# Another order of work in the gated stage, and norms that signal each tile

## The chip, the cores and the metric

The kernel runs on one core of a Trainium2 chip. The metric is the time of one execution on the device in microseconds (us), the median of several runs; the profile is of one execution of its own. The engines are TensorE (PE, with its weight loads as PEld), VectorE (DVE), ScalarE (ACT), GpSimd (POOL) and SyncE (SP, which here only issues DMAs). Each engine works through its own instructions in the order in which the program wrote them, and a semaphore wait at the head of a queue holds everything behind it.

## The reference

Eight sequences of 512 tokens with 128 channels pass through eight sub-layers, each added to the residual stream x after a norm: a slot attention, a mixture of low-rank experts, a polar attention, the experts again, an attention by distance, a feed-forward with squared relu, an attention with a learned Gaussian gate, and the feed-forward again. The change touches the stretch between the distance attention and the gated one:

```python
x = x + attn_a(layernorm(x))            # its last step: context @ W_o.T
x = x + ffn(layernorm(x))               # r = relu(h); (r * r) @ w_proj, h has 512 channels
x = x + attn_b(layernorm(x))            # the gated attention; prepared from:
mixed_q = y @ wq + bq ; mixed_k = y @ wk + bk ; mixed_v = y @ wv + bv
glo = mean(mixed_q over tokens)
c = tanh(mixed_q @ wfq + bfq + (glo @ wfg + bfg))
P = sigmoid(sum(c * up)) * 512 ; Z = sigmoid(sum(c * uz)) * 512
G = -(j - P) ** 2 * 2 / Z ** 2
```

## The kernel before, in words

The program has three groups: a slot phase, a middle group (polar, distance), and a last group with the gated stage, the gated attention and the last phase. The **gated stage** (`GatedPhase`, by its prefix d7 and its tiles e_...) prepares the gated attention. It goes by batches: a batch is one of the 8 sequences, a [128 x 512] block of four tiles of 128 tokens. It is a software pipeline of steps s = 0 to 11: in step s each engine works on batch s with the parts of lag 0 (called b0 here), on batch s-1 with the parts of lag 1 (b1), and so on (b2, b3, b4). The functions `tensor`, `scalar`, `vector`, `gpsimd` and `store` write out the order for one step on PE, ACT, DVE, POOL and SP; that order is fixed by hand.

What happens to one batch:

- lag 0: `out.turn` (L176, four PE transposes of the context), `out.copy` (L182, ACT), `out.project` (L188, PE), `out.add` (L194, DVE, into x), then the first norm: `statistics` (L228) and `aggregate` (L235) on DVE, `scale` on POOL (L241 and L242 on [128 x 4], L245 a power, L247 the shift), `normalise` (L254, four ACT instructions), `turn` (L262, four PE transposes) and `copy` (L268, ACT).
- lag 1: `ffn.hidden` (L396, four products, one bank each), `relu` (L401, ACT), `square` (L406: blocks 0 and 1 on DVE, 2 and 3 on POOL), `ffn.project` (L414, 16 accumulated products), `ffn.add` (L421, DVE), and the second norm, `norm2`, by the same lines as the first; then `query` (L668, PE), `mix_query` (L685, ACT, with a sum over the tokens), `key` (L672) and `globals` (L723, one column), both PE.
- lag 2: `query_high` (L691), `key_high` (L702) on ACT, `global_bias` (L729), `key_rest` (L707), `query_rest` (L696), `values` (L712) on DVE, `centre` (L718), `steepness` (L741), `value` (L677), `position` (L745) on PE, `centre_tanh` (L736) and the two `middle` (L445) on ACT, the two `low` (L449) on DVE. Each splits a float32 into three bfloat16 parts; SP stores them (L1244).
- lag 3: `steep` (L752, L755), `position_tanh` (L760), `distance` (L765), `curves_high` (L779) on ACT; `curves` (L772, L774) and `curves_rest` (L784, [128 x 1536]) on DVE.
- lag 4: `middle` and `low` of the curves (L445, L449 at [128 x 1536]), and seven stores by SP (L1250 to L1256). `curves_high` of batch b waits until the stores of batch b-2 have landed.

Before the change PE's order in a step is hidden(b1), centre(b2), ffn.project(b1), out.turn and out.project(b0), steepness, value, position(b2), norm2.turn and query(b1), norm.turn(b0), key and globals(b1). Next step's hidden reads what `norm.copy` of this step wrote. The eight PSUM banks are shared by name (`Banks`): `take` makes PE wait until the readers of the bank's former use are done, and the plan lists name, bank, lag and readers in PE's order. The norm's semaphore `xn_ready` is raised once for four tiles, and PE waits for it once.

Behind the stage, the gated attention needs its stacks filled (L1489, L1625, L1641, sprinkled over steps 7, 8 and 10) and loaded (L1463). Its first work on PE is L1539, on DVE L1658.

Of the kernel before, what the change touches and what calls it, by code (L numbers as in the profile page):

```python
# [17 lines left out]
NT = T // P  # L18
# [22 lines left out]
def wait_ge(eng, sem, value):  # L41

    if isinstance(value, int) and value <= 0:
        return
    eng.wait_ge(sem, value)
# [151 lines left out]
class Norm:  # L197
# [40 lines left out]
    def scale(self, pool, b):  # L238
        u = b % 2
        pool.wait_ge(self.mv_ready, b + 1)  # L240
        pool.tensor_scalar(self.vareps[:, u, :], self.meanvar[:, u, :, 1], EPS, None, ALU.add).then_inc(self.ve_ready, 1)  # L241
        pool.tensor_scalar(self.minus_mean[:, u, :], self.meanvar[:, u, :, 0], -1.0, None, ALU.mult)  # L242
        pool.wait_ge(self.ve_ready, b + 1)
        wait_ge(pool, self.xn_ready, b - 1)
        pool.tensor_tensor(self.rstd[:, u, :], self.vareps[:, u, :], self.sv.minus_half[:, 0:NT], ALU.pow).then_inc(self.rstd_ready, 1)  # L245
        pool.wait_ge(self.rstd_ready, b + 1)
        pool.tensor_tensor(self.shift[:, u, :], self.minus_mean[:, u, :], self.rstd[:, u, :], ALU.mult).then_inc(self.shift_ready, 1)  # L247

    def normalise(self, act, b):
        u = b % 2  # L250
        act.wait_ge(self.shift_ready, b + 1)
        wait_ge(act, self.turned, b - 1)
        for t in range(NT):
            last = act.activation(self.xn[:, u, t, :], self.sv.x[:, b * NT + t, :], ACT.Identity,  # L254
                                  bias=self.shift[:, u, t:t + 1], scale=self.rstd[:, u, t:t + 1])
        last.then_inc(self.xn_ready, 1)

    def turn(self, pe, b):
        pe.wait_ge(self.xn_ready, b + 1)
        to = self.banks.take(pe, self.bank, b)  # L260
        for t in range(NT):
            last = pe.transpose(to[:, t * P:(t + 1) * P], self.xn[:, b % 2, t, :], self.sv.ident[:, :])  # L262
        last.then_inc(self.turned, 1)

# [6 lines left out]
class Experts:  # L271
# [95 lines left out]
        last.then_inc(self.lora_done, 1)  # L367

    def bias(self, pool, b):
        pool.wait_ge(self.norm.xn_ready, b + 1)  # L370
        x = x_tiles(self.sv, b)
        pool.tensor_tensor(x, x, self.sv.base_bias[:, :].unsqueeze(1).to_broadcast([P, NT, D]), ALU.add).then_inc(self.bias_added, 1)

# [714 lines left out]
class GatedPhase:  # L1088
# [4 lines left out]
    def __init__(self, nc, sv, tag, wo, early, late, psum):  # L1093
        self.sv = sv
        out = self.out = OutProjection(early, sv, f"{tag}_o", wo)
        ffn_norm = Norm(early, sv, f"{tag}_n", "xnT", out.added)
        ffn = self.ffn = SquaredRelu(early, sv, f"{tag}_f", ffn_norm, last_hidden=1)
        norm, norm2 = self.norm, self.norm2 = ffn_norm, Norm(early, sv, f"{tag}_m", "xnT2")
        prep = self.prep = PrepareGated(late, sv, f"{tag}_p", norm2, early)
        norm2.x_ready = ffn.x_done  # L1100
        self.place = (4, 5, 6, 7, 0, 1, 2, 3)
        banks = self.banks = Banks(nc, tag, 8, (
            ("h2", 4, 1, (ffn.relu_done[2],)), ("h0", 2, 1, (ffn.relu_done[0],)), ("h3", 5, 1, (ffn.relu_done[3],)), ("h1", 3, 1, (ffn.relu_done[1],)),
            ("c", 5, 2, (prep.cT_ready,)), ("o", 1, 1, (ffn.x_done,)), ("ctx", 0, 0, (out.ctxT_ready,)), ("out", 1, 0, (out.added,)),
            ("z", 6, 2, (prep.ez_ready,)), ("v", 4, 2, (prep.v_ready,)), ("p", 7, 2, (prep.th_ready,)), ("xnT2", 0, 1, (norm2.xnT_ready,)),
            ("q", 2, 1, (prep.q_ready,)), ("xnT", 0, 0, (norm.xnT_ready,)), ("k", 3, 1, (prep.k_split.rest_ready,)), ("g", 5, 1, (prep.gb_ready,))), tensors=[psum[:, i, :] for i in self.place])
        out.banks = norm.banks = norm2.banks = ffn.banks = prep.banks = banks

    def bank_done(self, eng, place):
# [22 lines left out]
    def tensor(self, pe, s):  # L1132
        out, norm, norm2, ffn, prep = self.out, self.norm, self.norm2, self.ffn, self.prep
        for b in batch(s, 1):
            ffn.hidden(pe, b, 2)
            ffn.hidden(pe, b, 0)
            ffn.hidden(pe, b, 3)
            ffn.hidden(pe, b, 1)
        for b in batch(s, 2):
            prep.centre(pe, b)  # L1140
        for b in batch(s, 1):
            ffn.project(pe, b)
        for b in batch(s, 0):
            out.turn(pe, b)
            out.project(pe, b)
        for b in batch(s, 2):
            prep.steepness(pe, b)
            prep.value(pe, b)
            prep.position(pe, b)
        for b in batch(s, 1):  # L1150
            norm2.turn(pe, b)
            prep.query(pe, b)
        for b in batch(s, 0):
            norm.turn(pe, b)
        for b in batch(s, 1):
            prep.key(pe, b)
            prep.globals(pe, b)

    def scalar(self, act, s):
# [6 lines left out]
        for b in batch(s, 1):  # L1166
            ffn.relu(act, b, 2)
            ffn.relu(act, b, 0)
            ffn.relu(act, b, 3)
            ffn.relu(act, b, 1)  # L1170
        for b in batch(s, 3):
            prep.position_tanh(act, b)
            prep.distance(act, b)
        for b in batch(s, 2):
            prep.centre_tanh(act, b)
            prep.q_split.middle(act, b)
            prep.k_split.middle(act, b)
        for b in batch(s, 3):
            prep.curves_high(act, b)
        for b in batch(s, 0):  # L1180
            out.copy(act, b)
        for b in batch(s, 4):
            prep.c_split.middle(act, b)
        for b in batch(s, 1):
            norm2.normalise(act, b)
            norm2.copy(act, b)
        for b in batch(s, 0):
            norm.normalise(act, b)
        for b in batch(s, 1):
            prep.mix_query(act, b)  # L1190
        for b in batch(s, 0):
            norm.copy(act, b)

    def vector_start(self, dve):
        out, norm, norm2, ffn, prep = self.out, self.norm, self.norm2, self.ffn, self.prep
# [2 lines left out]
    def vector(self, dve, s):  # L1198
# [6 lines left out]
            ffn.square(dve, b, 1)  # L1205
        for b in batch(s, 2):
            prep.query_rest(dve, b)
        for b in batch(s, 3):
            prep.curves(dve, b)
        for b in batch(s, 2):  # L1210
            prep.q_split.low(dve, b)
            prep.k_split.low(dve, b)
        for b in batch(s, 1):
            ffn.add(dve, b)
            norm2.statistics(dve, b)
            norm2.aggregate(dve, b)
        for b in batch(s, 0):
            out.add(dve, b)
            norm.statistics(dve, b)
            norm.aggregate(dve, b)  # L1220
        for b in batch(s, 2):
            prep.values(dve, b)
        for b in batch(s, 3):
            prep.curves_rest(dve, b)
        for b in batch(s, 4):
# [1 line left out]

    def gpsimd(self, pool, s):
        out, norm, norm2, ffn, prep = self.out, self.norm, self.norm2, self.ffn, self.prep
        for b in batch(s, 1):  # L1230
            norm2.scale(pool, b)
        for b in batch(s, 0):
            norm.scale(pool, b)
            ffn.square(pool, b, 2)
            ffn.square(pool, b, 3)

# [1748 lines left out]
```

## Time and profile before

| | |
|---|---|
| median of 3 runs | 1828.64 us (1828.11 to 1833.12) |
| the profiled execution | 1834.62 us, of which the profile's span is 1832.8 us |
| mean granted TensorE clock | 0.929 of full |
| gated stage in the trace | 1174.3 us (first transposes) to 1370.7 us (first L1539); DVE begins on the attention at 1385.7 us |
| busy over the whole span | PE 88%, ACT 71%, DVE 67%, POOL 20% |

Times in the rows are microseconds from the start of the span. A row of the timeline gives the start, the time from the first start to the last end, the engine, line, operation, output<-inputs, and how many instructions were merged; in brackets, how long the engine was idle before them and who released it. A row of the windows gives the stretch, its length, then the busy time of PE, PEld, DVE, ACT and POOL, each with its number of instructions, the granted TensorE clock (1.00 is 2.4 GHz, 0.50 is 1.2 GHz), the DMA share and GB/s.

### The profile page before, as it was taken

How to read it: one execution, taken by the hardware profiler on the slowest of the kernel's cores; microseconds unless marked ns; L12 is line 12 of the kernel's file. 1: busy time of each engine (PE TensorE's matmuls, PEld its weight loads, DVE VectorE, ACT ScalarE, POOL GpSimd, SP SyncE). 2: the span in 40 equal slices, each digit the busy share in tenths (PEclk: the TensorE clock that was granted, in tenths of full speed). 3: DMA queues.
4: the chain of work that ended last, by engine and by line, in shares of the span. 5: the costliest groups of instructions: out<-in, count | busy, mean ns of one | idle time of the engine just before them, and what ended most of it. 6: DMA issues, size and time to landing. Idle time of an engine off the chain costs nothing. (4 is left out here: it accounts for less than half of the span.)

```text
span 1832.8 us, 39127 instructions
## 1 busy us (share of the span) xinstructions
PE 1614.7 (88%) x14558; PEld 777.7 (42%) x14558; DVE 1233.8 (67%) x2503; ACT 1296.0 (71%) x2201; POOL 364.1 (20%) x660
## 2 busy tenths in 40 slices
PE   7899996865899999986989999777766999999988
PEld 4676674751233333345633333255431333333356
DVE  4777777799899999947611111146668999999743
ACT  4655643784688888864789999657763888888863
POOL 3422423631000000013300000023330000000153
PEclk9899896985899999998989999889976999999999
DMA  4000000055222222200131111002233222222101
GB/s 123 1 1 1 1 1 1 1 159 173 67 71 77 79 75 71 71 2 10 57 87 57 57 57 56 1 18 62 83 101 88 63 60 56 61 61 61 29 7 41
DMA packets 115392, 98.51 MB, mean 54 GB/s; under 512 B 26762, under 2 KB 105412, under 8 KB 115204
## 3 DMA queue, kind: packets, MB, share of 16 engines
q1 hardware_dynamic: 114148, 95.68, 18.5%
q8 instruction: 117, 1.92, 0.4%
q14 instruction: 71, 0.58, 0.1%
q10 hardware_dynamic: 1056, 0.33, 0.1%
HBM read 63.82 MB, written 31.59 MB: 52 GB/s over the span
## 5 line engine op out<-in xcount | busy, mean ns | idle before, releaser
L1613 ACT ACTIVATE m_probs<-m_psum 128x512 f32<-128x512 f32 (+1 forms) x768 | 513.8, 758 | 98.1 <-PE m_psum L1530 92.6
L1613 ACT ACTIVATE e_probs<-e_psum 128x512 f32<-128x512 f32 x512 | 277.2, 597 | 84.3 <-PE e_psum L1530 78.6
L1658 DVE TENSOR_REDUCE a_minus_max<-m_psum 128x1 f32<-128x512 f32 x512 | 316.1, 682 | 17.8 <-PE m_psum L1539 12.5
L1658 DVE TENSOR_REDUCE a_minus_max<-e_psum 128x1 f32<-128x512 f32 x512 | 316.1, 682 | 12.7 <-PE e_psum L1539 6.7
L1530 PE MATMUL m_psum<-m_q_stack,m_k_stack 114*32 114x512 bf16 (+1 forms) x4096 | 295.4, 385 | 13.8 <-issue 7.1
L1550 PE MATMUL m_psum<-m_probs,m_v_ones 128*32 128x512 f32 x2048 | 271.0, 601 | 2.3 <-ACT m_probs L1613 1.6
L1530 PEld LDWEIGHTS m_psum<-m_q_stack,m_k_stack 114*32 114x32 bf16 (+1 forms) x4096 | 102.1, 96 | 218.9 <-issue 124.0
L1530 PE MATMUL e_psum<-e_q_stack,e_k_stack 126*32 126x512 bf16 x2048 | 158.4, 385 | 4.6 <-issue 2.5
L1502 POOL CAST a_max_parts<-a_minus_max 128x16 bf16<-128x16 f32 x64 | 12.6, 196 | 657.2 <-DVE a_minus_max L1658 657.2
L1550 PE MATMUL e_psum<-e_probs,e_v_ones 128*32 128x512 f32 x1024 | 133.3, 595 | 0.9 <-ACT e_probs L1613 0.8
L1539 PE MATMUL m_psum<-m_k_stack,m_q_stack 48*128 48x512 bf16 x512 | 113.3, 400 | 17.1 <-DVE a_minus_max L1658 17.0
L1539 PE MATMUL e_psum<-e_k_stack,e_q_stack 60*128 60x512 bf16 x512 | 113.0, 398 | 17.0 <-DVE a_minus_max L1658 16.8
L1603 DVE COPY m_ctxT<-m_psum 128x512 f32<-128x512 f32 x16 | 11.1, 691 | 173.0 <-PE m_psum L1550 173.0
L1530 PEld LDWEIGHTS e_psum<-e_q_stack,e_k_stack 126*32 126x32 bf16 x2048 | 43.4, 95 | 109.7 <-ACT e_probs L1613 63.4
L1550 PEld LDWEIGHTS m_psum<-m_probs,m_v_ones 128*32 128x32 f32 x2048 | 51.7, 110 | 69.0 <-ACT m_probs L1613 45.8
L1539 PEld LDWEIGHTS e_psum<-e_k_stack,e_q_stack 60*128 60x128 bf16 x512 | 29.5, 94 | 116.5 <-DVE a_minus_max L1658 88.4
L1539 PEld LDWEIGHTS m_psum<-m_k_stack,m_q_stack 48*128 48x128 bf16 x512 | 29.5, 94 | 115.5 <-DVE a_minus_max L1658 86.7
L1884 POOL TENSOR_TENSOR s_rope_product<-s_qkv,rope 128x512 f32<-128x512 f32 x32 | 40.3, 1287 | 158.6 <-ACT s_qkv L1849 158.6
L1495 POOL COPY m_v_ones<-vtok 128x128 f32<-128x128 f32 x64 | 18.6, 291 | 238.8 <-PE m_psum L1550 238.6
L1669 DVE RECIPROCAL m_inv<-m_psum 128x32 f32<-128x32 f32 x32 | 11.3, 352 | 59.2 <-PE m_psum L1558 59.2
L254 ACT ACTIVATE e_q_stack<-x,e_v_ones 128x128 f32<-128x128 f32 x64 | 26.3, 482 | 33.9 <-POOL e_v_ones L247 33.9
L2172 ACT ACTIVATE s_o<-s_bank 128x512 f32<-128x512 f32 x8 | 4.8, 597 | 59.8 <-PE s_bank L2165 59.8
(427 smaller groups left out, 2763.7 us busy)
## 6 DMA issues: line engine op xcount, KB each, us to landing
polar_q<-m_late SPq DMA_DIRECT2D x24, 256.0 KB, 3.0
polar_k<-m_late SPq DMA_DIRECT2D x24, 256.0 KB, 3.4
m_q_stack<-polar_q SPq DMA_DIRECT2D x64, 96.0 KB, 2.3
m_k_stack<-polar_k SPq DMA_DIRECT2D x64, 96.0 KB, 2.3
m_q_stack<-dist_parts SPq DMA_DIRECT2D x192, 32.0 KB
m_k_stack<-dist_parts SPq DMA_DIRECT2D x192, 32.0 KB
gate_parts<-e_late SPq DMA_DIRECT2D x24, 256.0 KB, 3.0
e_q_stack<-gate_parts SPq DMA_DIRECT2D x64, 72.0 KB
```

What stands on the lines that cost most here:

```text
L254: last = act.activation(self.xn[:, u, t, :], self.sv.x[:, b * NT + t, :], ACT.Identity, bias=self.shift[:, u, t:t + 1], scale=self.rstd[:, ...
L1495: pool.tensor_copy(self.buf.v_ones[n % 2][:, :, :, 16 * (n % 2):16 * (n % 2) + DH], self.sv.vtok[:, tiles_of(b), g * GW:(g + 1) * GW].rear ...
L1502: pool.tensor_copy(self.max_parts[:, 0, :], self.minus_max[n % 2][:, :]).then_inc(self.hi_ready, 1)
L1530: last = pe.matmul(self.ps_s[i % self.PAIRS][r:r + 32, j, :], self.buf.k_stack[g][0:self.rows, h, c * P + r:c * P + r + 32], self.buf.q_st ...
L1539: pe.matmul(to[:, :], self.buf.q_stack[g][part, h, t * P:(t + 1) * P], self.buf.k_stack[g][part, h, :], start=True, stop=True).then_inc(se ...
L1550: last = pe.matmul(self.ps_pv[32 * h:32 * h + self.buf.VW, :], self.buf.v_ones[m % 2][:, c, h, :], self.buf.probs[(NT * m + c) % self.buf. ...
L1603: copied = eng.tensor_copy(self.buf.ctxT[m // 2 % 2][:, :], self.ps_pv[:, :])
L1613: act.activation(self.buf.probs[(NT * m + c) % self.buf.PROBS][:, self.WIDE * part:self.WIDE * (part + 1), :], self.ps_s[i % self.PAIRS], ...
L1658: dve.tensor_reduce(self.minus_max[n % 2][:, k:k + 1], ps[:, :], AX.X, ALU.max, negate=True).then_inc(self.bank_free, 1)
L1669: dve.reciprocal(inv[:, :, :, :], raw[:, :, :, :, DH]).then_inc(self.inv_ready, 1)
L1884: pool.tensor_tensor(self.products[n][:, :, :, :], halves[:, :, :, i, :], table, ALU.mult).then_inc(self.rope_steps, 1)
L2172: act.activation(self.o2[b % 2][:, :], self.banks.of("o")[:, :], ACT.Square).then_inc(self.o2_ready, 1)
```

## The change

`Norm.normalise` raises `xn_ready` after each of the four tiles, and `Norm.turn` takes its bank first and waits for each tile before its transpose; the two other waits on `xn_ready` count by four. This holds for every norm of this class, in the last phase and the middle group too. `Norm.scaled` is new: a DVE wait for the shift. The rest is in `GatedPhase`:

- PE: out.turn(b0) and centre(b2) and then out.project(b0) stand ahead of ffn.project(b1); value ahead of steepness; query behind norm.turn.
- ACT: out.copy(b0) directly behind the relus; centre_tanh between position_tanh and distance; norm.normalise(b0) behind curves_high, ahead of the curves' middle(b4) and of norm2.normalise(b1); norm.copy ahead of mix_query.
- DVE: out.add, statistics, aggregate(b0) ahead of curves(b3) and of ffn.add(b1); key's low behind values and behind the new wait for norm2's shift, ahead of curves_rest.
- POOL: norm.scale(b0) ahead of norm2.scale(b1).
- Banks: "out" moves from bank 1 to 6 (behind z), "xnT" from bank 0 to 1 (behind o), and the plan follows PE's new order.

```diff
     def normalise(self, act, b):
         u = b % 2
         act.wait_ge(self.shift_ready, b + 1)
         wait_ge(act, self.turned, b - 1)
         for t in range(NT):
-            last = act.activation(self.xn[:, u, t, :], self.sv.x[:, b * NT + t, :], ACT.Identity,
-                                  bias=self.shift[:, u, t:t + 1], scale=self.rstd[:, u, t:t + 1])
-        last.then_inc(self.xn_ready, 1)
+            act.activation(self.xn[:, u, t, :], self.sv.x[:, b * NT + t, :], ACT.Identity,
+                           bias=self.shift[:, u, t:t + 1], scale=self.rstd[:, u, t:t + 1]).then_inc(self.xn_ready, 1)
 
     def turn(self, pe, b):
-        pe.wait_ge(self.xn_ready, b + 1)
         to = self.banks.take(pe, self.bank, b)
         for t in range(NT):
+            pe.wait_ge(self.xn_ready, NT * b + t + 1)
             last = pe.transpose(to[:, t * P:(t + 1) * P], self.xn[:, b % 2, t, :], self.sv.ident[:, :])
+    def scaled(self, dve, b):
+        dve.wait_ge(self.shift_ready, b + 1)
...
@@ GatedPhase.tensor
+        for b in batch(s, 0):
+            out.turn(pe, b)
         for b in batch(s, 2):
             prep.centre(pe, b)
+        for b in batch(s, 0):
+            out.project(pe, b)
         for b in batch(s, 1):
             ffn.project(pe, b)
-        for b in batch(s, 0):
-            out.turn(pe, b)
-            out.project(pe, b)
         for b in batch(s, 2):
+            prep.value(pe, b)
             prep.steepness(pe, b)
-            prep.value(pe, b)
             prep.position(pe, b)
         for b in batch(s, 1):
             norm2.turn(pe, b)
-            prep.query(pe, b)
         for b in batch(s, 0):
             norm.turn(pe, b)
         for b in batch(s, 1):
+            prep.query(pe, b)
             prep.key(pe, b)
             prep.globals(pe, b)
@@ GatedPhase.scalar
+        for b in batch(s, 0):
+            out.copy(act, b)
         for b in batch(s, 3):
             prep.position_tanh(act, b)
+        for b in batch(s, 2):
+            prep.centre_tanh(act, b)
+        for b in batch(s, 3):
             prep.distance(act, b)
...
         for b in batch(s, 3):
             prep.curves_high(act, b)
         for b in batch(s, 0):
-            out.copy(act, b)
+            norm.normalise(act, b)
         for b in batch(s, 4):
             prep.c_split.middle(act, b)
         for b in batch(s, 1):
             norm2.normalise(act, b)
             norm2.copy(act, b)
         for b in batch(s, 0):
-            norm.normalise(act, b)
+            norm.copy(act, b)
         for b in batch(s, 1):
             prep.mix_query(act, b)
-        for b in batch(s, 0):
-            norm.copy(act, b)
@@ GatedPhase.vector
         for b in batch(s, 2):
             prep.query_rest(dve, b)
+        for b in batch(s, 0):
+            out.add(dve, b)
+            norm.statistics(dve, b)
+            norm.aggregate(dve, b)
         for b in batch(s, 3):
             prep.curves(dve, b)
         for b in batch(s, 2):
             prep.q_split.low(dve, b)
-            prep.k_split.low(dve, b)
         for b in batch(s, 1):
             ffn.add(dve, b)
             norm2.statistics(dve, b)
             norm2.aggregate(dve, b)
-        for b in batch(s, 0):
-            out.add(dve, b)
-            norm.statistics(dve, b)
-            norm.aggregate(dve, b)
         for b in batch(s, 2):
             prep.values(dve, b)
+        for b in batch(s, 1):
+            norm2.scaled(dve, b)
+        for b in batch(s, 2):
+            prep.k_split.low(dve, b)
         for b in batch(s, 3):
             prep.curves_rest(dve, b)
@@ GatedPhase.gpsimd
+        for b in batch(s, 0):
+            norm.scale(pool, b)
         for b in batch(s, 1):
             norm2.scale(pool, b)
         for b in batch(s, 0):
-            norm.scale(pool, b)
             ffn.square(pool, b, 2)
             ffn.square(pool, b, 3)
```

## Rows read from the trace of the kernel before

**Rows 1.** Windows: steps 1, 2, 5 and 8 of the gated stage.
```profile
1185.05:1208.45 23.40, 17.08 (x66) 10.43 (x67) 5.34 (x20) 8.69 (x19) 5.41 (x10) 0.72 0.00 0
1208.45:1228.26 19.81, 16.70 (x82) 10.31 (x82) 8.81 (x26) 11.88 (x23) 5.41 (x10) 0.96 0.15 41
...
1271.17:1292.33 21.16, 16.07 (x84) 9.95 (x82) 14.31 (x30) 15.90 (x29) 7.87 (x10) 1.00 0.28 80
...
1335.72:1361.82 26.10, 18.12 (x67) 10.95 (x66) 14.10 (x23) 15.25 (x26) 7.98 (x8) 0.77 0.34 98
```

**Rows 2.** Timeline of step 5, PE, from the batch's hidden on.
```profile
1271.17 3.68 PE L396 MATMUL e_psum<-e_k_stack,ffn_fc 128*128 128x512 f32 x8
1274.90 1.10 PE L718 MATMUL e_psum<-e_probs,l1b_w 128*128 128x512 f32 x2
1276.99 3.81 PE L414 MATMUL e_psum<-ffn_proj,e_probs 128*128 128x128 f32 x32 [0.99 <-DVE e_probs L406]
1280.64 0.60 PE L176 MATMUL e_psum<-ident,ctx 128*128 128x128 f32 x4
1281.92 1.16 PE L188 MATMUL e_psum<-l1a_wo,e_ctxT 128*128 128x128 f32 x8 [0.69 <-ACT e_ctxT L182]
...
1286.49 0.66 PE L262 MATMUL e_psum<-ident,e_q_stack 128*128 128x128 f32 x4 [0.80 <-ACT e_q_stack L254]
1287.84 1.13 PE L668 MATMUL e_psum<-e_k_stack,l1b_w 128*128 128x512 f32 x2 [0.69 <-ACT e_k_stack L268]
1290.83 0.66 PE L262 MATMUL e_psum<-ident,e_q_stack 128*128 128x128 f32 x4 [1.87 <-ACT e_q_stack L254]
```

**Rows 3.** Timeline of the same step, ACT; the last row is of the next step.
```profile
1284.79 1.65 ACT L254 ACTIVATE e_q_stack<-x,e_v_ones 128x128 f32<-128x128 f32 x4 [1.55 <-POOL e_v_ones L247]
...
1287.19 0.60 ACT L268 ACTIVATE e_k_stack<-e_psum 128x512 f32<-128x512 f32 x1 [0.74 <-PE e_psum L262]
...
1289.13 1.65 ACT L254 ACTIVATE e_q_stack<-x,e_v_ones 128x128 f32<-128x128 f32 x4 [1.35 <-POOL e_v_ones L247]
1290.69 0.67 ACT L685 ACTIVATE pope_table<-e_psum,l1b_b 128x512 f32<-128x512 f32 x1
...
1294.37 2.28 ACT L401 ACTIVATE e_probs<-e_psum 128x512 f32<-128x512 f32 x4
```

**Rows 4.** Timeline of the same step, DVE and POOL.
```profile
1277.42 0.68 DVE L772 TENSOR_TENSOR e_late<-e_late 128x512 f32<-128x512 f32 x1
...
1280.84 0.69 DVE L421 TENSOR_TENSOR x<-e_psum,x 128x512 f32<-128x512 f32 x1 [0.81 <-PE e_psum L414]
...
1282.47 0.38 DVE L235 BATCH_NORM_AGGREGATE e_v_ones<-e_v_ones 128x2 f32<-128x6 f32 x4
...
1283.44 1.04 POOL L245 TENSOR_TENSOR e_v_ones<-e_v_ones,minus_half 128x4 f32<-128x4 f32 x1
...
1284.56 0.20 POOL L247 TENSOR_TENSOR e_v_ones<-e_v_ones 128x4 f32<-128x4 f32 x1
...
1285.62 1.75 DVE L784 TENSOR_TENSOR e_late<-e_late 128x1536 f32<-128x1536 f32 x1
1285.72 2.54 POOL L245 TENSOR_TENSOR e_v_ones<-e_v_ones,minus_half 128x4 f32<-128x4 f32 x1
```

**Rows 5.** Timeline of the tail: PE, ACT, DVE and SP, one engine after another.
```profile
1342.49 5.44 PE L414 MATMUL e_psum<-ffn_proj,e_probs 128*128 128x128 f32 x32 [1.00 <-DVE e_probs L406]
...
1357.48 2.07 PE L668 MATMUL e_psum<-e_k_stack,l1b_w 128*128 128x512 f32 x2 [0.69 <-ACT e_k_stack L268]
...
1379.04 1.48 ACT L779 ACTIVATE e_late<-e_late 128x1536 bf16<-128x1536 f32 x1 [6.92 <-DMA gate_parts<-e_late]
...
1371.61 1.75 DVE L449 TENSOR_TENSOR e_late<-e_late 128x1536 bf16<-128x1536 f32 x1
...
1373.39 1.81 SPq L1250 DMA_DIRECT2D gate_parts<-e_late  x3
```

**Rows 6.** Windows, PE alone: a stretch of step 6 with a lower clock.
```profile
1311.00:1315.50 4.50, 3.51 (x9) 0.64 0.64 197
```

More of the change, by code:

```diff
@@ L243, in scale @@
         pool.wait_ge(self.ve_ready, b + 1)
-        wait_ge(pool, self.xn_ready, b - 1)
+        wait_ge(pool, self.xn_ready, NT * (b - 1))
         pool.tensor_tensor(self.rstd[:, u, :], self.vareps[:, u, :], self.sv.minus_half[:, 0:NT], ALU.pow).then_inc(self.rstd_ready, 1)
@@ L369, in bias @@
     def bias(self, pool, b):
-        pool.wait_ge(self.norm.xn_ready, b + 1)
+        pool.wait_ge(self.norm.xn_ready, NT * (b + 1))
         x = x_tiles(self.sv, b)
@@ L1102, in __init__ @@
         banks = self.banks = Banks(nc, tag, 8, (
[L1103 to L1106, printed above, removed]
+            ("h2", 4, 1, (ffn.relu_done[2],)), ("h0", 2, 1, (ffn.relu_done[0],)), ("h3", 5, 1, (ffn.relu_done[3],)), ("h1", 3, 1, (ffn.relu_done[1],)), ("ctx", 0, 0, (out.ctxT_ready,)), ("c", 5, 2, (prep.cT_ready,)), ("out", 6, 0, (out.added,)), ("o", 1, 1, (ffn.x_done,)), ("v", 4, 2, (prep.v_ready,)), ("z", 6, 2, (prep.ez_ready,)), ("p", 7, 2, (prep.th_ready,)), ("xnT2", 0, 1, (norm2.xnT_ready,)), ("xnT", 1, 0, (norm.xnT_ready,)), ("q", 2, 1, (prep.q_ready,)), ("k", 3, 1, (prep.k_split.rest_ready,)), ("g", 5, 1, (prep.gb_ready,))), tensors=[psum[:, i, :] for i in self.place])
         out.banks = norm.banks = norm2.banks = ffn.banks = prep.banks = banks
@@ L1170, in scalar @@
             ffn.relu(act, b, 1)
+        for b in batch(s, 0):
+            out.copy(act, b)
         for b in batch(s, 3):
             prep.position_tanh(act, b)
+        for b in batch(s, 2):
+            prep.centre_tanh(act, b)
+        for b in batch(s, 3):
             prep.distance(act, b)
         for b in batch(s, 2):
-            prep.centre_tanh(act, b)
             prep.q_split.middle(act, b)
```

## The prediction

> **What bounds the kernel now.** I read the windows by step first, then one steady step on every engine, then the chain's end of the stage.
>
> The gated stage is about 200 of 1834 us, and the change's own work is all in it. [rows 1] show that no engine is full there: in step 5, at a full granted clock of 1.00 (2.4 GHz), PE is busy 16.07 us of 21.16, ACT 15.90, DVE 14.31, POOL 7.87. So the step is a chain of waits, not an engine's throughput. I count t from the start of hidden (1271.17). The chain in [rows 2 to 4], for batch b1: ffn.project runs from t = 5.82 (1276.99), when the squares are done, ffn.add starts at 9.67, aggregate ends at 11.68, POOL has the shift at 13.59 (1284.56 + 0.20), normalise runs 13.62 to 15.27, the four transposes start at 15.32, norm2.copy runs 16.02 to 16.62. I call the end of norm2.copy T.
>
> Then comes what the step pays for b0. After T the next hidden starts only at 21.16, which is T + 4.54. In between, the first norm's normalise starts at 17.96 (1289.13) because its POOL scale, second in POOL's queue, took 2.54 us for the power instead of 1.04 [rows 4]; its transposes start at 19.66 with PE idle for 1.87 us before them [rows 2]; mix_query stands behind that normalise on ACT and starts only at 19.52 [rows 3]. Query itself was done at about 17.8. The reader is to see two norms run one behind the other where b0's has no need to wait for b1's.
>
> **The change part by part.**
>
> **1. PE's detour ahead of ffn.project (a loss).** PE finishes hidden at 3.73 (next start, [rows 2]), then transposes the context (0.60) and runs centre (1.10): free at about 5.3. The relus of a step start 2.04 after hidden (1294.37, hidden at 1292.33) and take 2.28, so out.copy (0.60, the duration of the L268 row of the same shape) follows at 4.3 to 4.9. Out.project (1.16, pitch to the next 1.0) then holds PE to 6.1 to 6.3, against 5.82 where the squares are ready. I take +0.3 for ffn.project; ends 0 and 0.5. Its cover is squaring, which is the later event today.
>
> **2. DVE's order (a loss for b1).** Squares end at 5.7, query_rest (0.7) at 6.3. Out.add needs out.project (6.3); add, statistics, aggregate take 2.01 (1280.84 to 1282.85, [rows 4]) and end at 8.35. Curves are two instructions of 0.7 (0.68, [rows 4]), 9.75; the query's low 0.65, 10.4. Only then ffn.add: 10.4 against 9.67, aggregate ends at 12.4, POOL's 1.82 (12.5 to 14.3) gives norm2's shift at 14.3, against 13.59. With project at +0.5 the queue is still the later of the two, so this term is +0.7 either way.
>
> **3. POOL and the shared reads.** Norm.scale(b0) now runs from 8.45, beside the curves and a low, which all read two SBUF tensors. [rows 4] price that: the same power instruction takes 1.04 beside DVE's work from PSUM and statistics, and 2.54 when it starts 0.1 after L784, a DVE instruction with two SBUF operands. Without a conflict the shift is there at 8.35 + 0.1 + 1.82 = 10.3. At worst its reads get through only when the low ends at 10.4, then 0.95 for the power and 0.2: 11.7. In return DVE could slip a little. I take 11.7, the row that is nearest. The new DVE wait (scaled) keeps key's low, curves_rest and the curves' low away from norm2.scale. Behind that wait on DVE are 0.65 + 1.7 + 1.7 us, from 14.3 to about 18.3; the next thing DVE has to do (global_bias) cannot come before the next step, so the wait is covered by 1 us. Should that cover go, global_bias and with it the bank of h3 come late. SP's six stores of q and k then wait for key's low (15.0 instead of about 9) and go before the seven of the curves; those end near t = 4 of the next step and curves_high, which needs them, is at 9.8, so this costs nothing.
>
> The Trainium skill (SBUF — State Buffer, "Who interferes with whom") says that a DVE instruction with two SBUF inputs and a GpSimd instruction that reads SBUF exclude each other for the whole of whichever came first. The 2.54 agrees. By this rule the first scale ends at 11.7; read without it, at 10.3, and the period below would be 0.4 shorter.
>
> **4. ACT's order.** Curves_high starts when the curves are there, 9.8, with pitch 1.4: 11.2. Norm.normalise(b0) then starts at 11.7 (or 11.2), four tiles with pitch 1.56 in all: 13.25; the curves' middle 1.4: 14.65. So norm2.normalise(b1) starts at 14.65 (or 14.3, bound by POOL), against 13.62: +1.0, the largest loss.
>
> **5. Signals by tile (a gain).** From the start of four transposes to norm2.copy it is 0.70; with three done ahead, the last needs about a quarter of the 0.66, so 0.35. Gain 0.35. I give three more signals on ACT nothing: the relus signal each and run at a pitch of 0.56. In the middle group and the last phase norms are not at the head of the chain; nothing there.
>
> So T = 16.62 + 1.0 - 0.35 = 17.3.
>
> **6. Behind T (the gain).** Norm.turn has run before T. Query starts at T + 0.05 and takes 1.13, mix_query starts at T + 1.25 and signals after its sum at about T + 2.0; key is done by then; globals, and hidden at T + 2.25, not T + 4.54. ACT has norm.copy (0.5 pitch) before mix_query, in the shadow of query. The next relus start 3.68 - 0.5 = 3.2 after mix_query, 0.1 later against hidden than now. Period: 17.3 + 2.25 + 0.1 = 19.6 instead of 21.16, saving 1.55.
>
> **7. Steps of another kind.** Step 0 has only the signals by tile; the core comes there from a wait, and at half the clock (1.2 GHz) the 0.35 doubles: 0.7. Step 1 (23.40, clock 0.72) has no curves, low or middle; project is 0.9 or more late, tiles give 0.4 back, the two norms no longer queue: 1.0. Step 2 (19.81): T unchanged, hidden 2.25 behind it instead of 3.1: 1.1. Steps 3 to 7: 5 x 1.55 = 7.8. Step 8 (26.10, clock 0.77) has no b0. There norm2's scale met L784 too, costing about 2.0 with its shift instruction; PE then idled, and query ran at 2.07 instead of 1.13 [rows 5], and project took 5.44 instead of 3.81 at a lowered clock. The wait `scaled` takes the 2.0 away. Of the slow clock (1.6 + 0.9) I count on half, and ACT's middle no longer matters: 4.2 for this step up to its mix_query; ends 2.5 and 5.6.
>
> **8. Tail.** DVE reaches the attention at 1385.7 through curves_high of batch 7 (1379.04), which waited for the stores of batch 5, issued from 1373.39 behind a low at 1371.61 [rows 5]. That low waited behind values, and values behind steepness on PE. With value ahead of steepness it can be 1.3 us earlier; but the q and k stores, which now wait for key's low, keep SP busy to about 0.8 before today's. Gain 0.8; ends 0 and 2.
>
> **Sum:** 0.7 + 1.0 + 1.1 + 7.8 + 4.2 + 0.8 = 15.6 us. Against the profiled execution: 1834.62 - 15.6 = 1819.0. That execution is 6 us above the median of the runs; I take the 15.6 off the median, 1828.64: **1813.0**.
>
> **The rivals.**
>
> **A, the losses are mostly avoided (1807).** First scale not held up (period 19.2, 5 x 2.0), step 8 at full clock (5.6), tail 2: 0.7 + 1.3 + 1.4 + 10 + 5.6 + 2 = 21. For: PE idles less in all (16.1 of 19.6). Against: the 2.54 row.
>
> **B, the queues in front of norm2.normalise cost more (1821).** If POOL's conflict holds each of the four small instructions for one DVE instruction, or DVE is held by POOL in return, norm2.normalise slips by another 0.7: 5 x 0.85 = 4.3, steps 0 to 2 1.4, step 8 at slow clock 2, tail 0: 7.7. For: three in-order queues (DVE, POOL, ACT) now put b0 ahead of the critical b1. Against: each has slack of 0.3 to 0.5 in the walk above. If it slips by 1.5, the change gives nothing in steps 3 to 7 and the total is within 0.3%.
>
> **C, slower: the clock falls in the new gap (1836).** PE is done with position at about 12.9 and gets norm2's first tile at 15.1, one gap of 2.2 us where there were 0.8 and 1.87. In step 6 the granted clock was 0.64 right behind a gap of 1.87 [rows 6]. If it fell there in every step, query and key would take 2.07 each [rows 5], so that hidden comes 2.0 later, and hidden would be stretched like project (5.44 for 3.81), by 1.6: 3.6 us a step. Steps 2 to 7 then lose 3.6 - 1.55 = 2.05 each, 12.3, less 0.7 + 1.0 + 2.5 + 0.8 = 5.0 elsewhere: +7.3. It decides from a cost of about 2.4 a step. For: that step 6. Against: step 6 lost only 1.2 us, step 5 had the same gap at 1.00, and PE's busy share rises from 76 to 82%.
>
> The Trainium skill (TensorE: Matmul & The Clock Gate, Part 1) says that the engine's clock is at half unless recent activity released it; every step would be C if that gap were enough. Step 5's 1.00 speaks against it.
>
> **How the numbers follow.** Forecast 0.55, A 0.14, B 0.20 (of it 0.06 within 0.3%), no visible change for other reasons 0.04, C 0.07. A measurement of this kernel tells 0.3% (5.5 us) from no change: faster 0.83, same 0.10, slower 0.07. The range reaches from a little beyond A, 1804, to beyond B, 1823; what lies outside is C, no change, and a tail of A.
>
> **What would show it.** Steady step (hidden to hidden) 19.6 us; ffn.project about 6.1 after hidden; norm2.normalise about 14.6; norm.turn already run before norm2.copy's end; hidden 2.25 behind that end; the first L245 of a step near 2 us or more, the second 1.04; step 8 near 22 with its L245 at 1.04; attention's first L1658 some 15 us earlier. Wrong, if norm2.normalise starts past 16, if PE's clock is below 0.9 in steps 3 to 7, or if the gain of the stage is lost in the attention behind it.

## The result and the profile after

The changed kernel takes 1816.64 us (median of 5 runs, 1812.31 to 1817.17) against 1833.12 us (1828.11 to 1837.67) for the kernel before in the same comparison: a ratio of 0.991, with a 95% interval of 0.9886 to 0.9935. The profiled execution took 1817.17 us (span 1815.4), the one before 1834.62. The forecast was a gain of 15.6 us; the medians differ by 16.5, the profiled executions by 17.45. As a time it was 1813.0, counted from a median of 1828.64; in this comparison the kernel before stands 4.5 us higher, and the changed one 3.6 above the forecast. Two executions of the study, one of the kernel before (2896.83 us) and one of the kernel with query's low moved (3026.01 us), stand far above all others and are left out of every figure below.

A table of the same marks in both traces, from starts in the timeline (hidden to hidden; step 8 to the last centre; tail from there to DVE's first reduction for the attention):

| | step 0 | 1 | 2 | 3 | 4 | 5 | 6 | 7 | 8 | tail | stage |
|---|---|---|---|---|---|---|---|---|---|---|---|
| before | 10.77 | 23.40 | 19.81 | 21.99 | 20.92 | 21.16 | 22.32 | 21.07 | 26.10 | 23.87 | 211.4 |
| after | 10.30 | 21.52 | 19.96 | 20.15 | 20.43 | 20.42 | 20.42 | 20.42 | 19.97 | 25.39 | 199.0 |
| gain | 0.5 | 1.9 | -0.1 | 1.8 | 0.5 | 0.7 | 1.9 | 0.7 | 6.1 | -1.5 | 12.4 |

Of the 17.45 us, 12.4 are in the stage. The stage also began 5.2 us earlier (1169.0 instead of 1174.3), and behind it the two traces agree to 0.3 us (447.4 and 447.1). The nine kernels profiled here with the changed kernel's code ahead of the stage reached it between 1163.7 and 1170.3, a scatter of 6.6 us, and the profiled execution of before was itself 1.5 us over the median of its own comparison and 4.7 over that of the next. But that scatter lies in the first 800 us alone, and the 5.2 us can be taken apart. The marks are the first context transposes of the distance stage (PE, L176) and the first copy of the distance attention (DVE): in the kernel before, in the changed one, and in the changed one when PE waits for all four tiles at once (its experiment follows).

```profile
797.53 0.66 PE L176 MATMUL m_psum<-ident,ctx 128*128 128x128 f32 x4
941.16 0.69 DVE L1603 COPY m_ctxT<-m_psum 128x512 f32<-128x512 f32 x1 [20.96 <-PE m_psum L1550]
...
794.72 0.66 PE L176 MATMUL m_psum<-ident,ctx 128*128 128x128 f32 x4
935.91 0.69 DVE L1609 COPY m_ctxT<-m_psum 128x512 f32<-128x512 f32 x1 [21.06 <-PE m_psum L1556]
...
793.13 0.66 PE L176 MATMUL m_psum<-ident,ctx 128*128 128x128 f32 x4
936.74 0.69 DVE L1609 COPY m_ctxT<-m_psum 128x512 f32<-128x512 f32 x1 [20.90 <-PE m_psum L1556]
```

From mark to mark it is 143.63 us before, 141.19 changed and 143.61 without the waits by tile; in all ten kernels that have them it is 141.1 to 141.7. From the second mark to the gated stage it is 233.1 in all twelve. So 2.4 of the 5.2 us are a gain of the signals by tile in the distance stage. The other 2.8 stand before the first mark, which the nine kernels with the same code reach between 789.1 and 795.9, and can't be told from scatter. I count 12.4 + 2.4 = 14.8 as the change's.

The windows of the changed kernel, steps 1, 2, 5 and 8 and the tail, answer to [rows 1] (the same columns):

```profile
1179.34:1200.86 21.52, 16.15 (x66) 10.13 (x67) 5.36 (x20) 8.42 (x18) 5.41 (x10) 0.75 0.00 0
1200.86:1220.82 19.96, 17.58 (x84) 10.72 (x82) 8.78 (x26) 12.60 (x24) 5.75 (x10) 0.91 0.15 41
...
1261.40:1281.82 20.42, 17.53 (x81) 10.81 (x82) 13.95 (x30) 15.79 (x29) 6.83 (x10) 0.92 0.29 83
...
1322.66:1342.63 19.97, 15.77 (x65) 9.07 (x66) 13.23 (x23) 14.60 (x25) 5.93 (x8) 0.93 0.40 113
1342.63:1368.00 25.37, 6.36 (x18) 3.35 (x18) 14.26 (x16) 15.90 (x20) 2.95 (x6) 0.63 0.44 127
```

Steps 4 to 7 now have the same length, but at a granted clock of 0.92 where step 5 was at 1.00; PE is busy 17.53 us for the work that took 16.07. The timeline of step 5 (t from 1261.40), the PE rows that answer to [rows 2]:

```profile
1261.40 3.79 PE L398 MATMUL e_psum<-e_k_stack,ffn_fc 128*128 128x512 f32 x8
...
1266.36 1.16 PE L188 MATMUL e_psum<-l1a_wo,e_ctxT 128*128 128x128 f32 x8
1267.35 3.74 PE L416 MATMUL e_psum<-ffn_proj,e_probs 128*128 128x128 f32 x32
...
1272.68 1.02 PE L747 MATMUL e_psum<-e_probs,l1b_up 128*128 128x512 f32 x2
1276.23 1.83 PE L264 MATMUL e_psum<-ident,e_q_stack 128*128 128x128 f32 x8 [2.53 <-ACT e_q_stack L257]
1278.31 1.73 PE L670 MATMUL e_psum<-e_k_stack,l1b_w 128*128 128x512 f32 x2 [0.25 <-ACT e_k_stack L270]
1279.83 1.92 PE L674 MATMUL e_psum<-e_k_stack,l1b_w 128*128 128x512 f32 x2
1281.53 0.42 PE L725 MATMUL e_psum<-e_late,l1b_w 128*128 128x1 f32 x2
1281.82 3.81 PE L398 MATMUL e_psum<-e_k_stack,ffn_fc 128*128 128x512 f32 x8
```

The eight transposes of both norms (L264) are one row: norm.turn directly behind norm2.turn. Query and key, 1.13 and 1.02 at the full clock, take 1.73 and 1.92 behind the gap of 2.53 us. The POOL and ACT rows of the same step, for [rows 3, 4]; L245 is the power, L257 normalise, L447 (1.47) the curves' middle:

```profile
1269.66 0.58 POOL L241 TENSOR_SCALAR e_v_ones<-e_v_ones 128x4 f32<-128x4 f32 x1 [3.33 <-DVE e_v_ones L235]
...
1270.31 0.64 POOL L242 TENSOR_SCALAR e_v_ones<-e_v_ones 128x4 f32<-128x4 f32 x1
...
1270.92 1.44 POOL L245 TENSOR_TENSOR e_v_ones<-e_v_ones,minus_half 128x4 f32<-128x4 f32 x1
...
1272.68 1.65 ACT L257 ACTIVATE e_q_stack<-x,e_v_ones 128x128 f32<-128x128 f32 x4 [0.29 <-POOL e_v_ones L247]
...
1273.99 1.04 POOL L245 TENSOR_TENSOR e_v_ones<-e_v_ones,minus_half 128x4 f32<-128x4 f32 x1
1274.23 1.47 ACT L447 ACTIVATE e_late<-e_late 128x1536 bf16<-128x1536 f32 x1
...
1275.61 1.63 ACT L257 ACTIVATE e_q_stack<-x,e_v_ones 128x128 f32<-128x128 f32 x4
```

The first scale is held up in three instructions (0.58, 0.64, 1.44 for 0.24, 0.23, 1.04), the second in none. Norm2's normalise (1275.61) stands directly behind the middle, and its shift had been ready since 1275.30.

### The profile page after: what moved, and what is told of

The parts are those of the page before. It is cut to its first block and busy times, and to the rows that moved or that the text cites. A ratio compares the mean times of both kernels' runs of the same rounds, so it can differ in the third digit from the quotient of the medians.

```text
span 1815.4 us, 39134 instructions
## 1 busy us (share of the span) xinstructions
PE 1620.8 (89%) x14558; PEld 777.5 (43%) x14558; DVE 1233.2 (68%) x2503; ACT 1295.1 (71%) x2201; POOL 359.2 (20%) x660
## 3 DMA queue, kind: packets, MB, share of 16 engines
q8 instruction: 117, 1.92, 0.4%
## 5 line engine op out<-in xcount | busy, mean ns | idle before, releaser
L1664 DVE TENSOR_REDUCE a_minus_max<-e_psum 128x1 f32<-128x512 f32 x512 | 316.0, 684 | 13.2 <-PE e_psum L1545 11.7
L1536 PE MATMUL m_psum<-m_q_stack,m_k_stack 114*32 114x512 bf16 (+1 forms) x4096 | 295.3, 385 | 14.8 <-issue 6.9
L1675 DVE RECIPROCAL m_inv<-m_psum 128x32 f32<-128x32 f32 x32 | 11.3, 354 | 58.9 <-PE m_psum L1564 58.9
L257 ACT ACTIVATE e_q_stack<-x,e_v_ones 128x128 f32<-128x128 f32 x64 | 26.3, 481 | 22.7 <-POOL e_v_ones L247 22.7
```

Source lines behind the costliest of these rows:

```text
L1536: last = pe.matmul(self.ps_s[i % self.PAIRS][r:r + 32, j, :], self.buf.k_stack[g][0:self.rows, h, c * P + r:c * P + r + 32], self.buf.q_st ...
L1664: dve.tensor_reduce(self.minus_max[n % 2][:, k:k + 1], ps[:, :], AX.X, ALU.max, negate=True).then_inc(self.bank_free, 1)
```

## The experiments

**The two halves of the change.** One kernel has the signals alone (against the kernel before; the instruction's operands and the waits that count by four are left out here):

```diff
-        last.then_inc(self.xn_ready, 1)
+            act.activation(...).then_inc(self.xn_ready, 1)
+            pe.wait_ge(self.xn_ready, NT * b + t + 1)
```

> The kernel before with one part of the change alone: each of the four tiles signals and the transposes wait tile by tile, in every norm of this class; the order of the gated stage is the old one. Theory (the signals shorten each norm by 0.35 us at the head of a chain, nothing outside the gated stage): the gated stage, first context transposes to the attention's first DVE reduction, shrinks from 211.4 by 2 to 4 us, the stretch ahead of the stage stays at 1174 within its own scatter of a few us. Rival (the 5.2 us by which the changed kernel reached the stage earlier came from the signals in the slot and middle groups): the stage starts at about 1169 here too, and the total is 7 to 9 us below before.

The other has the new order alone (against the changed kernel):

```diff
     def turn(self, pe, b):
+        pe.wait_ge(self.xn_ready, NT * (b + 1))
         to = self.banks.take(pe, self.bank, b)
         for t in range(NT):
-            pe.wait_ge(self.xn_ready, NT * b + t + 1)
```

> The changed kernel, but PE waits for all four tiles before the first transpose; the new order alone. Theory: the gated stage is 3 to 4 us longer than the 199.0 of the changed kernel (0.4 in each of eight steps, since norm2's transposes then start 1 us later and end 0.35 later), and a steady step takes 20.8 instead of 20.42. Rival (the transposes spread over the normalise are what keep or lose TensorE's clock): the step changes by more than 0.6 either way, and the granted clock of the query with it.

Measured: signals alone 1825.94 us, ratio 0.997 (0.9958 to 0.9981), stage 209.1; order alone 1823.12 us, ratio 0.9953 (0.9937 to 0.9969), stage 202.0 with steady steps of 20.5. The stage's gains of 2.3 and 9.4 add up to 11.7 of the 12.4, but the 2.3 is not 0.35 a step. In the old order the signals gave 5.9 us in steps 0, 1, 2 and 8, and steps 3 to 7 became 3.6 us longer together, at granted clocks of 0.87 to 0.93 where the kernel before had 0.94 to 1.00. Its step 5:

```profile
1263.20 4.19 PE L395 MATMUL e_psum<-e_k_stack,ffn_fc 128*128 128x512 f32 x8
...
1279.46 1.12 PE L667 MATMUL e_psum<-e_k_stack,l1b_w 128*128 128x512 f32 x2 [0.69 <-ACT e_k_stack L267]
1281.71 1.54 PE L261 MATMUL e_psum<-ident,e_q_stack 128*128 128x128 f32 x4 [1.13 <-ACT e_q_stack L254]
1283.05 1.92 PE L671 MATMUL e_psum<-e_k_stack,l1b_w 128*128 128x512 f32 x2
...
1285.04 5.21 PE L395 MATMUL e_psum<-e_k_stack,ffn_fc 128*128 128x512 f32 x8
```

Query starts 16.26 behind hidden, 0.41 earlier than in [rows 2], but key takes 1.92 instead of 1.02 and the next hidden comes 5.58 behind query instead of 4.49. In the new order the signals give nearly nothing in a steady step (20.52 against 20.42) and 2.05 in step 8, 0.9 in step 1.

The first kernel reached the stage at 1168.1, the second at 1169.9. By these two starts alone the rival on the 5.2 us can't be judged; by the stretch of the distance stage it is right for 2.4 us, and the theory's "nothing outside the gated stage" is wrong: that stretch is 141.16 with the signals alone and 143.61 with the order alone. For the second the stage came out 3.0 longer as expected, but the 20.8 for its step was wrong: its queries take 2.07 where the changed kernel's take 1.73, so the two differ in the clock as well as in the signals, and neither my theory nor its rival names how the clock divides a step.

**The norm put back.** This undoes one move of the order, on ACT:

```diff
         for b in batch(s, 3):
             prep.curves_high(act, b)
-        for b in batch(s, 0):
-            norm.normalise(act, b)
         for b in batch(s, 4):
             prep.c_split.middle(act, b)
         for b in batch(s, 1):
             norm2.normalise(act, b)
             norm2.copy(act, b)
         for b in batch(s, 0):
+            norm.normalise(act, b)
             norm.copy(act, b)
```

> The changed kernel with one thing undone on ACT: the first norm's normalise stands behind norm2's copy again, not behind curves_high. Theory (the gain of the order is that b0's normalise and transposes are done before norm2's copy): norm2.normalise starts 0.4 earlier (13.8 after hidden), but after the copy query waits for 1.6 + 0.35 of norm and transposes; the step is 1 to 2 us longer than 20.42 with the clock as it is, about as long as before the change (21.2 to 22), stage about 209. Rival (the gain came from the context's projection moved ahead of the feed-forward's product): the step stays within 0.4 of 20.42.

Measured: 1829.32 us, ratio 0.9997 (0.9986 to 1.0008), stage 212.1, 3 us more than expected, steady steps 22.1 to 22.3. With everything else in place the stage's gain is gone, so the rival falls. This kernel does not price the projection's move alone, since query here also waits for the first norm's transposes, which it did not before the change; it shows that the other moves are worth nothing without b0's normalise in a time in which ACT would wait. Part of its loss can be the clock: key takes 1.46 to 1.92 in its steady steps.

**The new wait on DVE.** The call of `norm2.scaled` is left out; what it kept apart may meet.

```diff
         for b in batch(s, 2):
             prep.values(dve, b)
-        for b in batch(s, 1):
-            norm2.scaled(dve, b)
         for b in batch(s, 2):
             prep.k_split.low(dve, b)
```

> The changed kernel without DVE's new wait for norm2's shift. Theory (the wait keeps DVE's instructions with two SBUF inputs away from norm2's scale on POOL): key's low and curves_rest then run beside it, its power takes 2 to 2.8 us instead of 1.04, norm2's normalise starts 1 to 2 us later, a steady step takes 21.5 to 22.5 instead of 20.42, stage 199.0 + 7 to 12. Rival (the shared reads do not matter where ACT is the later): norm2.normalise is already 0.5 us behind its shift, so the step moves by less than 0.5.

Measured: 1820.65 us, ratio 0.9942 (0.9924 to 0.996), stage 203.2: 4.2 us longer, steady steps 20.8 to 21.8. The right sign, below the expected 7 to 12; steps 3 to 7 lose 3.9, step 8 loses 2.4 and the tail gains 2.4. Its POOL rows for norm2's scale:

```profile
1275.16 1.48 POOL L245 TENSOR_TENSOR e_v_ones<-e_v_ones,minus_half 128x4 f32<-128x4 f32 x1
1276.71 0.76 POOL L247 TENSOR_TENSOR e_v_ones<-e_v_ones 128x4 f32<-128x4 f32 x1
```

The power costs 0.44 more and the shift 0.56 more, not the 1.0 to 1.8 I had taken from the 2.54 of [rows 4]: first comes key's low of 0.69, not a DVE instruction of 1.75. What an instruction on POOL loses is what is left of the DVE instruction it meets. Norm2.normalise had 0.3 of slack, so some 0.7 a step is what one expects, and 0.35 to 1.36 is what the five steps show.

**The gap and the clock.** TensorE repeats the position product in the gap ahead of norm2's transposes, into the same bank with the same operands, twice:

```diff
     def position(self, pe, b):
         to = self.banks.take(pe, "p", b)
+        for _ in range(2):
+            pe.matmul(to[:, :], self.sv.l1b_up[:, 0, :], self.cT[b % 2][:, :], start=True, stop=True)
         pe.matmul(to[:, :], self.sv.l1b_up[:, 0, :], self.cT[b % 2][:, :], start=True, stop=True).then_inc(self.p_done, 1)
```

> The changed kernel with two repeats of the position product ahead of the real one (same operands, same bank), which fill 1.7 of the 2.53 us in which TensorE waits ahead of norm2's transposes. Theory (the gap costs the clock: query 1.73 instead of 1.13, key 1.91 instead of 1.02): the clock stays at 1.00, the end of norm2's copy to the next hidden shrinks from 3.56 to about 2.3, a steady step takes 19.2, total 6 to 9 us below the changed kernel. Rival (the clock falls whatever stands there): step unchanged at 20.4 and total within 2 us, or slower by what the repeats delay.

and once, with `range(1)`:

> The changed kernel with one repeat of the position product, which fills 0.86 of the 2.53 us gap and leaves 1.67. Theory (the gap ahead of norm2's transposes decides on the clock, and one of 1.7 is short enough, as the gaps of 1.9 of the kernel before mostly were): step 19.3 as with two repeats. Rival (any gap over about one microsecond costs the clock here): query 1.5 or more in most steps, step 20 or more.

Measured with two: 1810.79 us, ratio 0.9887 (0.9866 to 0.9908), stage 192.8, steady steps 19.04 to 19.29. With one: 1817.3 us, ratio 0.9917 (0.9902 to 0.9932), stage 199.1, steady steps 20.43. The PE timelines, two repeats:

```profile
1268.18 1.83 PE L264 MATMUL e_psum<-ident,e_q_stack 128*128 128x128 f32 x8 [0.94 <-ACT e_q_stack L257]
1270.26 1.12 PE L670 MATMUL e_psum<-e_k_stack,l1b_w 128*128 128x512 f32 x2 [0.25 <-ACT e_k_stack L270]
1271.22 1.02 PE L674 MATMUL e_psum<-e_k_stack,l1b_w 128*128 128x512 f32 x2
```

and one repeat:

```profile
1273.90 1.83 PE L264 MATMUL e_psum<-ident,e_q_stack 128*128 128x128 f32 x8 [1.67 <-ACT e_q_stack L257]
1275.98 1.71 PE L670 MATMUL e_psum<-e_k_stack,l1b_w 128*128 128x512 f32 x2 [0.25 <-ACT e_k_stack L270]
1277.49 1.91 PE L674 MATMUL e_psum<-e_k_stack,l1b_w 128*128 128x512 f32 x2
```

With two, the gap is 0.94 and query and key are at the full clock; with one it is 1.67, and they are as slow as with 2.53. The theory holds for the cause (work in the gap buys the clock, and the clock is 1.14 us of each step), and the rival won on the dose. Step 8 became 1.0 longer with two repeats (21.00), with query at 1.53 and key at 1.91 behind a gap of only 0.31. The length of one gap doesn't decide: in steps 3 to 7 of the kernel before, the key behind a gap of 1.87 ran at 1.02 in three steps and at 1.92 in one, and behind a gap of 1.31 at 1.91; with the signals alone it ran at 1.91 to 1.92 in all five, behind gaps of 1.13 at most. What does decide stays open.

**The queue of SP.** The loads for the attention's second group go behind the stores of step 9:

```diff
                 for s in range(gated.STEPS):
                     gated.store(sp, s)
                     if s == NB - 1:
                         gated.parts_stored(sp, 0)
-                    for u in FILLS.get(s, ()):
-                        attention.load(sp, u)
+                        attention.load(sp, 0)
+                    if s == NB + 1:
+                        attention.load(sp, 1)
+                    if s == NB + 2:
+                        attention.load(sp, 2)
+                        attention.load(sp, 3)
```

> The changed kernel with the loads for the attention's second group of stacks issued by SP in step 9 behind the stores of batch 7 and 5, no longer in step 8 ahead of them. Theory (the tail is bound by SP's queue: the store of the curves of batch 5 is issued 2.9 us after they are ready): curves_high of batch 7 and the attention's first DVE reduction come 2.5 to 3 us earlier after step 9's centre, 25.4 becomes about 22.6, and the total falls by 2 to 3 us. Rival (the loads are merely moved, and the attention waits for them): the attention starts earlier, but gives all of it back in its first groups, total within 0.5 us.

Measured: 1811.96 us, ratio 0.9897 (0.9879 to 0.9915), stage 196.7: 2.3 us off the changed kernel's, and nothing of it given back behind (447.3). Of this, 1.7 are in the tail (23.68), less than the 2.5 to 3 expected; the store of the curves of batch 5 is issued 11.3 us behind the last centre instead of 13.0. The 0.7 in step 8 are not SP's: query starts 16.53 behind hidden in both kernels, key then takes 1.02 instead of 1.91, and SP's order differs only behind this step. The timelines of the changed kernel's tail, DVE, then SP, then ACT, show why:

```profile
1350.97 1.75 DVE L451 TENSOR_TENSOR e_late<-e_late 128x1536 bf16<-128x1536 f32 x1
...
1345.53 1.28 SPq L1469 DMA_DIRECT2D e_q_stack<-gated_q  x3
...
1349.46 2.20 SPq L1469 DMA_DIRECT2D e_k_stack<-gated_k  x6
1351.76 1.84 SPq L1250 DMA_DIRECT2D gated_k<-e_late  x3
1353.70 1.84 SPq L1250 DMA_DIRECT2D gated_q<-e_late  x3
1355.64 1.85 SPq L1256 DMA_DIRECT2D gate_parts<-e_late  x3
...
1361.38 1.48 ACT L781 ACTIVATE e_late<-e_late 128x1536 bf16<-128x1536 f32 x1 [8.43 <-DMA gate_parts<-e_late]
```

The curves of batch 5 are ready when L451 ends at 1352.72; their stores are issued from 1355.64, because SP first issues 16 loads and six stores without a pause (22 DMAs from 1345.53 on). ACT's curves_high waits for them until 1361.38. In the kernel before, SP waited for DVE here, not the other way round [rows 5].

**Query's low moved.** First on the changed kernel alone, then with all that had helped:

```diff
             prep.curves(dve, b)
-        for b in batch(s, 2):
-            prep.q_split.low(dve, b)
...
             prep.k_split.low(dve, b)
+            prep.q_split.low(dve, b)
```

> The changed kernel with query's low moved behind key's low, no repeats. Theory (POOL's power meets that low and ACT passes it on; with it gone norm2.normalise starts 0.3 to 0.4 earlier, as it did together with the repeats, where the step fell from 19.29 to 18.88): step 20.0, stage 3 us below 199.0. Rival (the lowered clock behind the gap takes it back): norm2.normalise starts earlier, but query is 2.07 instead of 1.73 and the step stays at 20.3 to 20.5.

Measured: 1813.77 us (median of three), ratio 0.99 (0.988 to 0.992), stage 196.1, 2.9 less than the changed kernel's; steady steps 18.53 once, else 19.92 to 20.15. Stage and step come out as the theory said, but query is at 2.07 in three of those steps (1.12 in the one of 18.53, behind a gap of 2.02), as the rival said: both are at work.

The two repeats and SP's order together:

> The changed kernel with the two repeats of the position product and with the attention's second loads issued behind the stores. Theory (two separate causes, clock and SP queue, add up): steps 19.3 as with the repeats alone, tail 23.7 as with the loads alone or a little less, stage 191 to 192, total about 8 us below the changed kernel, ratio to before 0.986 to 0.988. Rival (one cover takes the place of the other): total as with the repeats alone.

Measured: 1808.45 us, ratio 0.9879 (0.9862 to 0.9895), stage 191.5, tail 23.65; one steady step of the five is 20.38, with query at 1.55 and key at 1.91 behind the same gap of 0.95 as in the others. Against the repeats alone the tail is 1.4 shorter, which is SP's part, and step 8 is 1.1 shorter, with key at 1.02 instead of 1.91; in the median it is 2.3 us better, across two comparisons.

All three, query's low included:

> As the one before, and query's low moved from between curves and the feed-forward's add to behind key's low. Theory (POOL's power for the first norm takes 1.44 instead of 1.04 because it meets that low, and ACT passes this on to norm2.normalise): the power falls to 1.04 to 1.2, norm.normalise and norm2.normalise start 0.3 earlier, step 19.0, stage 2 to 3 us below the one before. Rival (curves_high on ACT is as late as the shift): step 19.3 unchanged, and the later stores of q cost 0.6 in the tail.

Measured: **1803.49 us**, ratio 0.985 (0.9833 to 0.9867), stage 187.6, 3.9 below the one before (1.1 of it is what that kernel's one long step lost), steady steps 18.64 once, then 18.87 to 18.89. This is the fastest kernel of the study. Its POOL and ACT rows:

```profile
1266.19 1.03 POOL L245 TENSOR_TENSOR e_v_ones<-e_v_ones,minus_half 128x4 f32<-128x4 f32 x1
...
1267.56 1.63 ACT L257 ACTIVATE e_q_stack<-x,e_v_ones 128x128 f32<-128x128 f32 x4
1269.09 1.47 ACT L447 ACTIVATE e_late<-e_late 128x1536 bf16<-128x1536 f32 x1
1270.47 1.63 ACT L257 ACTIVATE e_q_stack<-x,e_v_ones 128x128 f32<-128x128 f32 x4
```

The power is back at 1.03, and ACT runs normalise, middle and normalise without a wait between them (the rows have no bracket). The curves on DVE, for which curves_high waits, and ACT's work behind them now set the start of norm2's normalise.

## Why the prediction was right, point by point

- **PE's detour (part 1).** Taken +0.3 for ffn.project, measured 5.95 against 5.82: 0.1. The out.project fits between relus and squares.
- **DVE's order (part 2).** Ffn.add was put at 10.4 and came at 9.99, directly behind the low; norm2's shift at 14.3, measured 13.90. Right in kind, 0.4 too late.
- **Shared reads (part 3).** First shift at 11.7, measured 11.24: the scale took 2.98 us (1269.66 to 1272.64) against the 1.82 free of DVE; I had 3.25 (8.45 to 11.7). The two late experiments confirm the cause: without the low beside it the power is 1.03, and without `scaled` norm2's power and shift grow by 1.0.
- **ACT's order (part 4).** Norm2.normalise at 14.65, measured 14.21, and it waits for the middle, as walked through.
- **Signals (part 5): a term wrongly put at nothing.** "In the middle group and the last phase norms are not at the head of the chain; nothing there" holds behind the stage (447.4 against 447.1) and not in the middle group: the distance stage is 2.4 us shorter. One place shows how, before and after:

```profile
842.38 1.12 PE L262 MATMUL m_psum<-ident,m_late 128*128 128x128 f32 x4 [15.39 <-ACT m_late L254]
843.29 1.06 PE L352 MATMUL m_psum<-ident,m_late 128*128 128x128 f32 x4
...
837.85 1.54 PE L264 MATMUL m_psum<-ident,m_late 128*128 128x128 f32 x4 [14.33 <-ACT m_late L257]
839.17 1.06 PE L354 MATMUL m_psum<-ident,m_late 128*128 128x128 f32 x4
```

  The transposes wait there for a normalise on ACT that starts at 840.70 and at 837.22, so the product behind them comes 2.59 us after its start before and 1.95 after. In the gated stage 0.35 a step was expected; alone in the old order the signals gave 2.3 us, and in steps 3 to 7 nothing, against a lower clock.
- **Behind T (part 6): the term that was mis-sized.** T came at 16.86 (I had 17.3), but the next hidden 3.56 behind it, not 2.25. The step is then 20.42 instead of 19.6 and steps 3 to 7 gave 5.6 us, not 7.8; step 2 gave -0.1, not 1.1. The 1.3 us are query and key at the lowered clock; with two repeats, and the clock full, hidden came 2.3 behind T. This is rival C's mechanism, in every step as it said, but at less than its price: I had 3.6 a step, with hidden stretched by 1.6; hidden in fact took 3.81 for 3.68, since the clock was back by then. I weighed C as a case of its own at 0.07, where it was a part of the forecast's case.
- **Step 8 (part 7).** 4.2 expected up to mix_query. Counted so, it is 23.87 (1359.59) against 17.74 (1340.40): 6.1. `scaled` kept the power at 1.04, and project ran at the full clock (3.81, against 5.44 in [rows 5]). I had counted on half of that clock. This is rival A's case for this step. The 4.2 itself was not fully worked out: the parts it names are 2.0 and half of 2.5, which is 3.25.
- **Tail (part 8).** 0.8 gained expected, 1.5 lost measured from the last centre. Value ahead of steepness did bring curves_rest and the low forward, but the step that failed is "SP to about 0.8 before today's": I let SP begin step 9's stores on time, and did not see that a shorter step 8 pushes its 13 stores into the 16 loads of the second group.

In the sum, errors met: 3.5 us too much in steps 2 to 7 (clock), 2.3 in the tail (SP) and 0.2 in step 0, against 1.9 too little in step 8 and 0.9 in step 1. The stage gave 12.4, not 15.6; another 2.4 came from the distance stage, for which the sum had nothing. So the order's mechanism was right, and that 15.6 lies so near the 16.5 of the medians is in good part luck: terms too high by 6.0 met terms too low by 2.8 and one that was left out. The medians' 16.5 confirm the sign and the order of size, not the last microseconds.

## What to carry to other kernels

In a hand-ordered pipeline, look for a chain whose inputs are ready and that stands in a queue behind a chain that waits; put it into the wait, and check each queue it then holds up. The same move closes some gaps of TensorE and joins others into one. Here the length of the gaps didn't foretell the clock, so put a loss of clock into the sum as a case of the forecast itself, read the granted clock of a steady step afterwards, and try idle work for TensorE in the gap. A stage that gets shorter meets queues of fixed length, here SP's DMA issues of 0.3 to 0.6 us each: count those of neighbours too. And where a change touches a class that other stages use, compare their stretches in the traces, between marks behind the part that scatters.

## What the runs showed of the hardware that I had not expected

- Two repeated products of 0.86 us in a gap of TensorE made a step 1.14 us shorter. With gaps of at most 0.95 us query and key ran at the full clock in nine of the ten steady steps of the two kernels that have the repeats alone or with SP's order, with gaps up to 1.67 and 2.53 in none. But the old order kept it in three of four steps over gaps of 0.8 and 1.87, and lost it in all five over gaps of 0.69 and at most 1.13 once the transposes followed tile by tile. What decides was not settled.
- A POOL instruction on [128 x 4] that meets a DVE instruction with two SBUF inputs is late by nearly the rest of that instruction: 0.40 us where 0.55 were left of one of 0.68, 1.50 where 1.65 were left of one of 1.75. The Trainium skill (SBUF — State Buffer, "Who interferes with whom") tells of this exclusion, and the traces agree; no slower DVE instruction was seen in return in this stage's curves (0.66 and 0.69, against 0.68 and 0.69 in the kernel before).
